# Gated delta net: first chunk without its zero-state products, gate products moved into the triangular inversions

## The reference

```python
def step(S, inp):                       # one token, S starts as zeros
    qt, kt, vt, bt, gt = inp
    S = S * jnp.exp(gt)[..., None, None]
    kv = jnp.einsum('bhk,bhkv->bhv', kt, S)
    delta = (vt - kv) * bt[..., None]
    S = S + jnp.einsum('bhk,bhv->bhkv', kt, delta)
    ot = jnp.einsum('bhk,bhkv->bhv', qt, S)
    return (S, ot)
...
g = (hidden_states @ Wg).reshape(b, l, NH, DV)
var = jnp.mean(o * o, axis=-1, keepdims=True)
o = o * jax.lax.rsqrt(var + 1e-05) * g_norm_weight
o = o * g * jax.nn.sigmoid(g)
return o.reshape(b, l, VD) @ Wo
```

## Time and profile before

| | us |
|---|---|
| median of 3 runs | 2719.34 |
| lowest, highest | 2716.93, 2723.6 |
| the profiled execution | 2734.56 |
| its span | 2732.8 |
| first scores of batches 3 and 4 in it (L547) | 737.09, 1066.40 |

### The profile page before, as it was taken

How to read it: one execution, slowest core, us unless ns; L and a number is a source line. 1 busy time by engine, 2 the same in 40 slices (tenths; PEclk the granted TensorE clock), 3 DMA queues, 4 the chain that set the end, 5 groups by cost and what they waited for, 6 DMA issues and landing times.

```text
span 2732.8 us, 65917 instructions
## 1 busy us (share of the span) xinstructions
PE 2433.6 (89%) x24299; PEld 1680.0 (61%) x24299; DVE 1794.9 (66%) x4697; ACT 1455.4 (53%) x3129; POOL 825.4 (30%) x581
## 2 busy tenths in 40 slices
PE   3899988899898998989989899899988999889998
PEld 2456765477554775547745577456764567655676
DVE  3467864777737776478655776567864678636776
ACT  0466534755448554385544754457444665446643
POOL 3036210552105520065202542025320363104621
PEclk7999999999999999999999999999999999999999
DMA  8201132011310114001220113201122011220113
GB/s 260 105 1 22 17 99 79 4 20 17 106 71 7 23 21 139 28 13 19 72 108 5 18 17 101 80 1 19 19 98 80 1 20 18 97 80 3 21 16 102
DMA packets 226985, 138.31 MB, mean 51 GB/s; under 512 B 173567, under 2 KB 209799, under 8 KB 219431
## 3 DMA queue, kind: packets, MB, share of 16 engines
q1 hardware_dynamic: 208870, 125.48, 16.2%
q10 hardware_dynamic: 17780, 8.39, 1.1%
HBM read 95.10 MB, written 38.71 MB: 49 GB/s over the span
## 4 chain that ended last, share of the span: by engine, by line
PE 50%; DVE 18%; ACT 15%; issue 8%; DMA 6%; SPq 2%; POOL 2%; ACTq 0%; DVEq 0%; POOLq 0%
PE bank L914 7%; PE bank L699 4%; PE bank L509 4%; PE bank L690 3%; DVE small L1367 3%; PE bank L1013 3%; PE bank L622 3%; ACT arena L1638 3%; ACT arena L1637 2%; PE bank L952 2%; DVE blk_tx L1369 2%; ACT vq L1645 2%; PE bank L547 2%; DVE mx L1171 2%; PE bank L602 2%
## 5 line engine op out<-in xcount | busy, mean ns | idle before, releaser
L1925 POOL TENSOR_TENSOR arena<-upto,gk 128x1536 f32<-128x1536 f32 x32 | 88.1, 2754 | 682.8 <-DVE beta L1308 682.8
L1315 DVE SCALAR_TENSOR_TENSOR arena<-bank,conv,arena 128x510 f32<-128x510 f32 x320 | 237.1, 747 | 45.1 <-ACT arena L1638 26.1
L509 PE MATMUL bank<-mask_k,ident_bf 128*128 128x512 bf16 x976 | 250.8, 391 | 0.0
L1171 DVE TENSOR_REDUCE mx<-bank 128x2 f32<-128x768 f32 (+3 forms) x187 | 201.5, 1123 | 47.2 <-PE bank L548 46.1
L1917 POOL TENSOR_TENSOR arena<-arena 128x511 f32<-128x511 f32 x160 | 201.8, 1272 | 56.8 <-DVE arena L1315 56.8
L1601 ACT ACTIVATE arena<-bank 128x384 f32<-128x384 f32 (+1 forms) x384 | 168.5, 544 | 49.3 <-PE bank L607 49.2
L760 PE MATMUL bank<-h_pad,arena 128*128 128x512 f32 x320 | 165.6, 615 | 28.7 <-DVE arena L1315 21.8
L547 PE MATMUL bank<-vq 128*128 128x512 bf16 (+3 forms) x544 | 123.2, 313 | 55.3 <-issue 32.9
L1367 DVE TENSOR_TENSOR small<-blk_tx,blk 96x1 f32<-96x1 f32 (+14 forms) x480 | 142.8, 297 | 16.5
L1622 ACT ACTIVATE arena<-bank,b1e 128x512 f32<-128x512 f32 x128 | 87.8, 686 | 116.8 <-PE bank L690 111.6
L1276 DVE SCALAR_TENSOR_TENSOR arena<-bank,comb,arena 128x128 f32<-128x128 f32 x256 | 72.0, 344 | 114.9 <-PE bank L699 113.7
(11 more groups left out here) (300 smaller groups left out, 5912.1 us busy)
## 6 DMA issues: line engine op xcount, KB each, us to landing
vq<-q_rows SPq DMA_DIRECT2D x18, 1024.0 KB, 7.6
vq<-k_rows SPq DMA_DIRECT2D x18, 1024.0 KB, 10.9
arena<-w_bounce SPq DMA_DIRECT2D x16, 1024.0 KB, 6.0
q_rows<-qkp SPq DMA_DIRECT2D x81, 128.0 KB, 2.4
k_rows<-qkp SPq DMA_DIRECT2D x81, 128.0 KB, 2.4
arena<-wv_rows SPq DMA_DIRECT2D x8, 768.0 KB, 10.1
ogt<-wv_rows SPq DMA_DIRECT2D x8, 768.0 KB, 11.7
t_bounce<-blk_tx SPq DMA_DIRECT2D x32, 192.0 KB, 2.1
```

What stands on the lines that cost most here:

```text
L509: mm(PS[bank][:, :], ident_bf[:, :], mask_k[:, :, :].rearrange("p h w -> p (h w)"), start=True, stop=True)
L1171: V.reduce_max(dst, unit_scores(u), AX.X).then_inc(s_max, 1)
L1315: ins = V.scalar_tensor_tensor(a[:, k:T], ps[:, 0:T - k], conv[:, n, 3 - k:4 - k], a[:, k:T], ALU.mult, ALU.add)
```

## The change

1. Chunk 0 does without the zero state: its memset, `key_part(0)`, `query_part(0)`, `differences(0)`, ACT's 12 scalings and POOL's `decay_state(0)` are gone. `unknowns(0)` multiplies the inverse by v itself, and DVE's `outputs(0)` becomes copies.
2. The lists behind the first inversion change: `unknowns(0)` stands first, the transposes of chunk 2 next, and `mask(2)` behind `outputs(0)`.
3. Gate groups move into the inversions: gate 0's second and third group into the second inversion, gate 1's into the third, all three of gate 2 into the fourth, with `project(1)` in two pieces. They take the place of most dummies (17 fewer in each batch).
4. ACT's `gate(1)` moves from before the third inversion to behind it, and `gate(2)` from before the fourth to behind it, together with `gate(3)` between one pair of table loads. DVE's `project(0)` and `rms(1)` move behind the third inversion, ahead of `subst(3)`; `project(1)` moves into the fourth.
5. The banks of chunk 2's transposes and masks and of the gates, and some waits, change with it.

```diff
...
-        act_stages += [("gate", 1), ("rms", 1), ("levels", 2), ("query_part", 2), ("unknowns", 2), ("project", 1)]
...
+        act_stages += [("levels", 2), ("rms", 1), ("gate", 1), ("query_part", 2), ("unknowns", 2), ("project", 1)]
...
                     for s in range(8):
-                        keep_warm(3, {3: 4, 4: 2, 6: 2}.get(s, 0))
+                        if c < 2:
+                            if c and s in (1, 3):
+                                gate_group(0, 1 if s == 1 else 2)
+                            keep_warm(3, {3: 2 if c else 4, 4: 2, 6: 2}.get(s, 0))
+                        elif c == 2 and s in (3, 4):
+                            keep_warm(3, {3: 1, 4: 0}[s])
+                            gate_group(1, s - 2)
+                        elif c == 3 and s in (1, 3):
+                            project(1, range(0, 4) if s == 1 else range(4, HD))
+                        elif c == 3 and s in (4, 6, 7):
+                            gate_group(2, (4, 6, 7).index(s))
...
                 def key_part(c):
 
-                    pe.wait_ge(s_ready, at(b, s_ready, 2 * c + 1))
+                    pe.wait_ge(s_ready, at(b, s_ready, 2 * c))
...
-                    if c == 0:
-                        pe.wait_ge(v_tok, at(b, v_tok, NTOK))
-                    else:
-                        pe.wait_ge(gate_ready, at(b, gate_ready, NG * (c if c + 1 < NT else NT)))
+                    pe.wait_ge(gate_ready, at(b, gate_ready, NG * (c if c + 1 < NT else NT)))
+                    if c == 2:
+                        pe.wait_ge(wo_done, at(b, wo_done, 1))
                     state_products(c, NP, ks_ps, ks_banks)
...
+                    if c == 0:
+                        pe.wait_ge(x_zero, at(b, x_zero, 1))
+                        pe.wait_ge(v_scaled, at(b, v_scaled, 1))
+                        pe.wait_ge(lv_sb, at(b, lv_sb, L_SB))
+                        pe.wait_ge(v_tok, at(b, v_tok, NTOK))
+                        pe.sem_inc(qs_ps, NG)
                     for g in range(NG):
...
-                            last = mm(ps[:, j * P:(j + 1) * P], xw[:, h, :], rb[:, h, :], start=True, stop=True)
+                            known = rb[:, h, :] if c else v_all[:, 0, h, :]
+                            last = mm(ps[:, j * P:(j + 1) * P], xw[:, h, :], known, start=True, stop=True)
...
+                            if c == 0:
+                                V.tensor_copy(state[:, ns, :], su_banks[i][:, 0:n * DV].rearrange("p (n v) -> p n v", n=n)).then_inc(s_ready, 1)
+                                continue
...
+                        if c == 0:
+                            V.tensor_copy(ob[:, hs, :], low_banks[g][:, :].rearrange("p (h t) -> p h t", h=GH)).then_inc(o_ready, 1)
+                            continue
...
                 def gate_silu(c):
-                    nc.scalar.preload_act_table_set("silu_and_others")
+                    if c + 1 < NT:
+                        nc.scalar.preload_act_table_set("silu_and_others")
...
-                    nc.scalar.preload_act_table_set(EXP_LN)
+                    if c != 2:
+                        nc.scalar.preload_act_table_set(EXP_LN)
...
```

More of the change, by code:

```diff
@@ L409, in adaln_two_layers @@
                      ("tokens", 17), ("tokens", 18), ("tokens", 19)]
-        pe_stages += [("levels", 0), ("keys", 2), ("queries", 2), ("key_part", 0), ("mask", 2), ("unknowns", 0), ("query_part", 0),
-                      ("outputs", 0), ("gate_first", 0), ("gram", 2), ("attend", 2), ("gate", 0)]
+        pe_stages += [("levels", 0), ("unknowns", 0), ("keys", 2), ("queries", 2), ("outputs", 0), ("mask", 2),
+                      ("gate_first", 0), ("gram", 2), ("attend", 2)]
         pe_stages += [("levels", 1), ("keys", 3), ("queries", 3), ("key_part", 1), ("mask", 3), ("unknowns", 1), ("query_part", 1),
-                      ("outputs", 1), ("turn_out", 0), ("gram", 3), ("project", 0), ("attend", 3), ("gate_first", 1), ("gate", 1)]
+                      ("outputs", 1), ("turn_out", 0), ("gram", 3), ("project", 0), ("attend", 3), ("gate_first", 1)]
         pe_stages += [("levels", 2), ("key_part", 2), ("query_part", 2), ("unknowns", 2),
-                      ("outputs", 2), ("turn_out", 1), ("gate_first", 2), ("project", 1), ("gate", 2)]
-        pe_stages += [("levels", 3), ("enter_norm", 1), ("gate_first", 3), ("gate", 3), ("enter_qkv", 1),
+                      ("outputs", 2), ("turn_out", 1)]
+        pe_stages += [("levels", 3), ("enter_norm", 1), ("gate", 3), ("enter_qkv", 1),
                       ("key_part", 3), ("query_part", 3), ("unknowns", 3), ("outputs", 3),
@@ L1027, in turn_out, with project @@
                         last.then_inc(og_ps, 1)
[L1029 removed]
+                def project(c, lot=range(HD)):
                     ps = wo_bank(c)
[L1031 to L1032 removed]
+                    if lot.start == 0:
+                        pe.wait_ge(ogt_ready, at(b, ogt_ready, NG * (c + 1)))
+                    for h in lot:
                         last = mm(ps[:, 0:D], ogt[:, h, :], wo[:, h, :], start=(h == 0), stop=(h == HD - 1))
[L1034 removed]
+                    if lot.stop == HD:
+                        last.then_inc(wo_ps, 1)
                 walk = {"conv": convolve, "tile": tile, "direct": direct, "tokens": to_tokens, "keys": keys, "queries": queries, "mask": mask, "gram": gram, "attend": attend,
@@ L1286, in _ @@
                 layer_norm(2, xs)
-                V.memset(state[:, :, :], 0.0).then_inc(s_ready, 1)
                 dve.wait_ge(gb_ps, at(b, gb_ps, 1))
```

93 lines of the change are left out of this document (44 added, 49 removed).

## The result

The changed kernel takes 2774.80 us (median of 4 runs, 2770.12 to 2781.93), the kernel before 2721.47 (4 runs, 2716.93 to 2728.04). The ratio is 1.0192, 95% interval 1.0163 to 1.022. So it is slower by 53 us where 28 were forecast: the sign and the range (2708 to 2778) held, but the forecast had about half of the loss. The profiled executions differ by 43 us (2777.37 against 2734.56).

The account below looks back on a forecast made before the run. PE's queue is close to the bound, but hand-overs set a third of the end; what counts is when ACT starts qkf. The steps sum to +3.5 us a batch, +28 over eight: 2747 us, range 2708 to 2778.

Parts of the forecast that it names:

- PE's queue decides: Rival: the removed 7.4 us a batch count and cover the new waits, 2660 us; chance 0.16, in full or good part.
- Step A: First to second inversion: DVE's outputs(0) stands behind masks' exponentials and scales, and gram(2) waits for it; +1.6 us.
- Step B: In the second inversion: gate groups, a Silu and a table load precede ACT's round 3 copies; +2.2 us, sum 3.8.
- Step C: Third inversion: starts +2.6 us, waiting for attend(3)'s evictions; inside, a 1.13 us wait for DVE goes, leaving +1.4.
- Step D: Behind the third inversion: key_part(2) waits for ACT's Silus, +4.9 us; DVE's differences(2) +5.1; the later counts.
- Step E: Up to the fourth inversion: the 6.4 us ahead of it is gone, so it starts 1.2 us earlier than before.
- Steps F and G: Fourth inversion to qkf: project(1) and gate groups add 3.2 us, three more ACT Silus 1.5; qkf +3.5 in all.
- The clock rival: Rival: PE's clock falls in the new gaps of 4 and 3 us, losing 3 us a batch, 2771 us; chance 0.19.
- No change: Rival: terms of B and D each a third smaller, F hidden; −0.7 us a batch, 2714 to 2722 us; chance 0.13.
- The table load's drain: Note outside the sum: about 1.38 us per table switch would make steps B and D each 1.4 later, some 2769 us.

Follow-up runs that it names:

- zero_only: The kernel before with only the zero state's work left out, every list in its old order, gates and dummies as before; 2701.13 us, ratio 0.9847.
- scale_first: The changed kernel with ACT's key_scale(2) and query_scale(2) ahead of mask(2)'s exponentials, attend(2) waiting for all three; 2760.55 us, ratio 1.0071.
- warm: The changed kernel with dummies in its three new PE gaps: 9 before gate_first(0), 8 before the second inversion, 15 before key_part(2); 2786.12 us, ratio 1.0151.
- lv_warm: The changed kernel with the third inversion's eight dummies back beside its two gate groups; 2790.78 us, ratio 1.0178.
- no_dummies: The kernel before with the third inversion's eight dummies taken out and nothing else; 2748.02 us, ratio 1.0044.
- both_filled: lv_warm with 15 more dummies in the gap ahead of key_part(2), all hand-overs as in the changed kernel; 2766.29 us, ratio 1.0107.

## Why the prediction was right and wrong

- **What bounds the kernel, and the direction.** Right. The removal itself gains (zero_only 0.9847) and the new order loses more than that. The rival that PE's queue decides fell: PE stands 2.74, 2.26 and 3.94 us for other engines.
- **The step that failed** is that the sum prices the clock at nothing: in A gram and attend behind the gap, in C the inversion without its dummies, in D and E the state products behind the gap all count as at full clock. The steps below have the numbers.
- **Step A.** The mechanism is right and shown by scale_first. +1.6 was forecast and +2.1 measured in the shortest batches, +3.1 on average. The masks' end and the scales came as worked out: the last exponential to DVE's `dec` took 1.1. The error is the half clock behind the gap. It stretches a gate group by 0.9, which fills the wait of 1 forecast before gram, and gram and attend by 0.8, which was not in the sum. In warm, with these at full clock, the stretch is 35.11, +1.3.
- **Step B.** 8.62 against 8.4 forecast, from the inversion's start to ACT's copies. Right.
- **Step C.** The start of the third inversion came 2.8 later in the fourth batch (2.1 and 0.7), 2.6 forecast. But "Two groups and a dummy (2.2) replace eight dummies (2.1)" is the first place where the step failed. In PE time that is equal. In place it is not: the groups stand ahead of rounds 3 and 4, nothing at round 6, and in the last rounds the clock falls in six of eight batches of the changed kernel, ahead of the gap; `key_part(2)` then starts 17.2 to 17.6 us behind the inversion's start instead of 16.4. With the dummies back (lv_warm) no batch falls there, and no_dummies shows that taking them out alone does it in eight of eight, where the kernel before has three.
- **Step D.** The gap 3.94 against 4 forecast, both halves as late as each other. `key_part(2)` came 4.75 later (2.8 and 16.40 less 14.48), 4.9 forecast. What was not in the sum is the 2.1 us by which the state products behind it are slow (5.19 instead of 3.04). They are in all eight batches.
- **Step E.** −1.2 was forecast for the start of the fourth inversion. In that batch it was +0.4 (106.28 us behind the first inversion's start instead of 105.92). Nearly all of the difference of 1.6 lies behind `key_part(2)`: from there to the fourth inversion 12.9 was forecast (984.7 to 997.6), 14.55 measured (1336.94 to 1351.49), and 12.46 in both_filled, where the clock does not fall. So at full clock this step would have come out 0.4 below the forecast. The wait for ACT's copies before the outputs, 0.83 (0.47 before the change), is in these numbers.
- **Steps F and G.** From the fourth inversion to `qkf` 22.91 or 22.92 in every batch, 17.9 to 18.3 before in the three undisturbed batches: +4.6 in the batch of the rows, forecast 4.7. Right.
- **The clock rival.** Its sum, 2771, was nearest to the measured 2774.80, and I gave it 0.19 and priced the clock at nothing in the forecast. Time at half clock went from 131 to 233 us. I argued that the wait of 1.13 us that disappears, with the falls inside the third inversion, may pay part back. Those falls did not go (three of eight batches before, six after), but the half clock behind the fourth inversion did (3.0 us a batch to none). My "some gaps of 3 us were followed by no fall" stood on little: of the four gaps of 3.0 to 3.3 us inside a batch before, one (3.04, before 1728.51) has no half clock near it, and of two of 2.7 neither has. The Trainium skill, "TensorE: Matmul & The Clock Gate", section "HAM oscillation — how this bites in real kernels", pointed the right way with its waits between bursts; lv_warm agrees (granted 0.50 from within a gap of 3.94 us on), and warm adds a case without any wait.
- **What the 45 us of the profiles are made of,** an estimate from the stretches. At full clock the changed kernel's four would be 35.1 (warm), 39.3, 28.9 (both_filled) and 47.2, those of before 33.9, 38.6, 33.4 and 42.3: +2.3 a batch, 18 us, where 28 were forecast. The half clock costs the changed kernel 5.3 a batch (1.8, 0.9 and 2.6) and cost the kernel before 3.0 (1.7 and 1.3): +2.3, 18 us, where nothing was forecast. The last 8 us are the +1.0 of scores to first inversion, which is not explained. So the waits were forecast some 10 us too high, and by luck this hid a part of the 18 us of the clock.
- **Two sums of the prediction** are off by themselves. Its bounds as listed (0.8 less in B, 1.5 less in D, 0.5 either way in F, 1.1 more in D) make 0.7 to 5.1 a batch, not 1.5 to 5.2. And a third of B's 2.2 is 0.7, not the 1.5 taken off in the rival *No change*.
- **The table load's drain**, a note beside the sum, did not show: the Silus start 0.02 us after the load (1335.25 to 1335.27), as in the earlier trace rows, and the steps with a load (B, D, G) came out as without it.

Open: why the clock falls in the second inversion or just behind it in two of eight batches of the changed kernel, in four of lv_warm and of both_filled (which are the same up to there), in five of scale_first and in all of warm, and why zero_only has less half clock than before. I have no run that separates the causes. That the same pair measured 1.0192 and 1.0143 in two sessions fits such differences, but is not explained.

## What to carry to other kernels

When work is moved to fill waits, look at each engine whose list it is moved in, not only at the busiest one: a copy behind an exponential on another engine's list, or a table load at the end of an inversion, costs what PE then waits. Undo such a step on all its engines together before judging it, since two that are equally late hide each other. And dummies that keep PE busy are not replaced by the same amount of useful work at another place: measure the granted clock where they stood. Dummies put into a gap cost time themselves when the clock has already fallen ahead of it. Try a removal by itself in its old order first: here it gained 1.5%, and the new order turned that into a loss of 1.4 to 1.9%.

## What the runs showed of the hardware

The granted clock can fall while PE works without a gap. The sixth batch of the changed kernel, windows behind the third inversion's start at 1989.27 (columns as in the earlier trace rows), and the timeline of PE in them:

```profile
1996.50:2000.50 4.00, 3.98 (x104) 3.33 (x103) 3.52 (x16) 3.05 (x10) 0.00 (x0) 1.00 0.01 4
2000.50:2004.50 4.00, 2.22 (x22) 2.03 (x19) 3.55 (x14) 2.35 (x6) 0.00 (x0) 0.50 0.00 0
```

```profile
1998.54 1.61 PE L906 MATMUL bank<-arena 64*64 64x64 f32 x24
2000.17 2.55 PE L909 MATMUL bank<-arena,u 64*64 64x64 f32 x24
2006.66 4.94 PE L956 MATMUL bank<-state,vq 64*128 64x128 f32 x48 [3.94 <-issue]
```

PE is busy 3.98 of 4 us, with 32x32 and 64x64 products, and then the last round takes 2.55 us where it takes 1.58 at full clock, ahead of the gap.

Eight dummies of 0.26 us in an inversion of 12 us, with nothing else changed, made the difference between three of eight batches and all eight (before and no_dummies). And where the places behind the first inversion were filled (warm), the clock fell in the second inversion in eight of eight batches, against two in the changed kernel, so that a gain at one place was more than paid at the next: 36.94 to 35.87 us, then 40.22 to 43.56.
